# A decoder block on one core: preparation, values and loads of W2 in another order within the turns

## The reference

```python
x = x + attention(layernorm(x))           # 16 heads of 128, softmax over channels
x = x + xattn(layernorm(x), ctx, gamma)   # below
x = x + ffn(layernorm(x))                 # below

# xattn: q is (B, 512, 512), split in 8 heads of 64 rows; k = v = ctx, split the same way
qk = einsum('bhdq,bhdl->bhql', qh, kh) / sqrt(64)
ret = gamma * einsum('bhql,bhdl->bhdq', softmax(qk), vh)

# ffn: w1q, w3q (1365 x 512) and w2q (512 x 1365) are ternary: sign(w) or 0, times mean |w|
out = (silu(x @ w1q.T) * (x @ w3q.T)) @ w2q.T
```

## Time and profile before

| | |
|---|---|
| median of 3 runs | 1131.79 us (1130.19 to 1132.29) |
| the profiled execution | 1132.07 us |
| its span | 1130.2 us |
| mean granted clock of PE | 0.997 |
| busy: PE, PEld | 1111.2 us (98%), 940.3 us (83%) |
| busy: DVE, ACT, POOL | 731.0 us (65%), 542.2 us (48%), 478.3 us (42%) |
| PE's share of the chain that ended last | 89% |

### The profile page before, as it was taken

One profiled execution on the slowest core, in us unless ns is written; L12 is line 12 of the kernel. 1 busy time (PEld: TensorE's weight loads), 2 busy tenths in 40 slices (PEclk: granted clock), 3 DMA queues, 4 the chain that ended last, 5 costly groups with the idle time before them and its releaser, 6 DMA issues.

```text
span 1130.2 us, 15803 instructions
## 1 busy us (share of the span) xinstructions
PE 1111.2 (98%) x5804; PEld 940.3 (83%) x5804; DVE 731.0 (65%) x1357; ACT 542.2 (48%) x1129; POOL 478.3 (42%) x420
## 2 busy tenths in 40 slices
PE   8999999999999999999999999989999999999998
PEld 6888888878888888888888888878787878888886
DVE  7555547777757588866424434679867976787532
ACT  3556673324142376677514323267627753775130
POOL 0222327341332275664434030266627762875131
PEclk9999999999999999999999999999999999999999
DMA  7465553545433634212631022362113211310000
GB/s 242 161 184 188 183 180 122 166 126 172 124 121 126 206 96 141 84 38 94 240 112 45 30 100 61 135 176 65 48 44 114 58 48 57 113 47 2 38 1 37
DMA packets 54663, 122.19 MB, mean 108 GB/s; under 512 B 10057, under 2 KB 10057, under 8 KB 52538
## 3 DMA queue, kind: packets, MB, share of 16 engines
q1 hardware_dynamic: 54586, 121.18, 33.2%
HBM read 103.32 MB, written 17.84 MB: 107 GB/s over the span
## 4 chain that ended last, share of the span: by engine, by line
PE 89%; DVE 4%; POOL 2%; DMA 1%; issue 1%; ACT 1%; SPq 0%; POOLq 0%; DVEq 0%; ACTq 0%
PE bank L161 19%; PE bank L162 19%; PE bank L163 19%; PE bank L562 5%; PE bank L563 5%; PE bank L520 4%; PE bank L577 4%; PE bank L578 4%; PE bank L530 2%; PE bank L544 2%; PE bank L545 2%; PE bank L531 2%; DMA x1d<-x_scratch 1%; POOL kl L909 1%; POOL qst L913 1%
## 5 line engine op out<-in xcount | busy, mean ns | idle before, releaser
L562 PE MATMUL bank<-x3h,w 128*128 128x512 f32 (+2 forms) x368 | 143.0, 392 | 0.4 <-DVE x3l L839 0.3
L563 PE MATMUL bank<-x3l,w 128*128 128x512 f32 (+2 forms) x368 | 140.1, 384 | 0.0
L1419 ACT ACTIVATE yh<-bank 128x512 fp32r<-128x512 f32 x64 | 38.1, 600 | 209.9 <-PE bank L163 209.9
L2025 POOL TENSOR_TENSOR wal<-raw_a,wah 128x512 fp32r<-128x512 f32 x44 | 60.5, 1401 | 137.5 <-ACT wah L1441 137.5
L754 DVE TENSOR_REDUCE xmx<-bank 128x1 f32<-128x512 f32 x128 | 87.6, 686 | 42.7 <-PE bank L531 41.4
L919 POOL TENSOR_SCALAR pe_x<-pe_x,xri,gam 128x512 f32<-128x512 f32 x96 | 75.6, 788 | 88.6 <-DVE xri L758 85.6
L2030 POOL TENSOR_TENSOR wbl<-raw_b,wbh 128x512 fp32r<-128x512 f32 x64 | 87.6, 1393 | 36.1 <-ACT wbh L1462 35.9
L161 PE MATMUL bank<-wah,gh 128*128 128x512 f32 x256 | 102.6, 401 | 0.0
L161 PE MATMUL bank<-yh,rh 128*128 128x512 f32 x256 | 100.2, 391 | 0.8 <-DVE xacc L1887 0.8
L1717 DVE TENSOR_TENSOR yl<-bank,yh 128x512 fp32r<-128x512 f32 x64 | 44.1, 691 | 86.8 <-ACT yh L1419 86.6
L162 PE MATMUL bank<-wal,gh 128*128 128x512 f32 x256 | 100.1, 391 | 0.0
(11 more groups left out here) (168 smaller groups left out, 2990.2 us busy)
## 6 DMA issues: line engine op xcount, KB each, us to landing
raw_a<-in_wk SPq DMA_DIRECT2D x8, 1024.0 KB, 5.6
raw_b<-in_wq SPq DMA_DIRECT2D x8, 1024.0 KB, 6.7
raw_a<-in_wo SPq DMA_DIRECT2D x8, 1024.0 KB, 5.2
raw_b<-in_wvt SPq DMA_DIRECT2D x8, 1024.0 KB, 5.2
ternary_scratch<-wraw SPq DMA_DIRECT2D x24, 341.2 KB, 3.0
x1d<-x_scratch SPq DMA_DIRECT2D x48, 128.0 KB, 2.9
kd<-in_ctx SPq DMA_DIRECT2D x48, 128.0 KB, 2.9
w<-ternary_scratch SPq DMA_DIRECT2D x2, 2730.0 KB, 10.9
```

Source lines behind the costliest of these rows:

```text
L562: pe.matmul(u_bank[w][0:m, cols], lhs, x3h[:, c, cols], start=c == 0, stop=False)
L563: mm = pe.matmul(u_bank[w][0:m, cols], lhs, x3l[:, c, cols], start=False, stop=c == CK - 1)
L2025: pool.tensor_tensor(wal[:, c, :], raw_a[:, c, :], wah[:, c, :].bitcast(F32), ALU.subtract).then_inc(s["wal_pool"], 1)
```

## The change

`prep_step` becomes 4h for all heads: head 3 is prepared at step 8 instead of 9, head 7 at 24 instead of 25, each with its second half (`act_queries`, `pool_prep`) one step later as before. `values_step` becomes 1, 10, 18 and 26 instead of 1, 8, 17 and 24, and POOL's low parts come at 2, 11, 19 and 27. In turn 1, SP issues W2 behind head 2's rows and ahead of the wait for vd. All instructions stay, only their places change.

```diff
         def values_step(h):
-            return 4 * h + (h % 4 == 0)
+            return 4 * h + 2 if h else 1
         def prep_step(h):
-            return 4 * h + (h % 4 == 2) if 0 < h < XH - 1 else None
+            return 4 * h if 0 < h < XH - 1 else None
...
+        def sp_vd(sp, m, b, h):
+            if h or b > 1:
+                sp.wait_ge(s["vtl"], b * V_TILES + h // 2)
+            sp.dma_start(m.vd[:], rows(ctx_cols, b)[h // 2]).then_inc(s["vd_in"], 16)
+
-        def sp_head(sp, m, b, h):
+        def sp_head(sp, m, b, h, values=True):
...
-            if h % 2 == 0 and b > 0:
-                if h or b > 1:
-                    sp.wait_ge(s["vtl"], b * V_TILES + h // 2)
-                sp.dma_start(m.vd[:], rows(ctx_cols, b)[h // 2]).then_inc(s["vd_in"], 16)
+            if h % 2 == 0 and b > 0 and values:
+                sp_vd(sp, m, b, h)
...
-            sp_head(sp, main, 1, 2)
+            sp_head(sp, main, 1, 2, values=False)
             sp_w2(sp)
+            sp_vd(sp, main, 1, 2)
...
-                    if values_step(h // 2 * 2) == n - 1:
-                        pool_vt(pool, main, b, h // 2 * 2)
+                    if n - 1 in map(values_step, range(0, XH, 2)):
+                        pool_vt(pool, main, b, (n - 1) // 8 * 2)
```

## The result

The changed kernel takes 1120.07 us (median of 4 runs, 1119.48 to 1123.63), the kernel before 1131.97 beside it: a ratio of 0.9905, 95% interval 0.9892 to 0.9919, so 11.9 us or 1.1% less. The prediction was 1121.8, with 10.1 us less. The profiled execution has a span of 1118.8 us, 11.4 less than before.

What follows compares the result with a forecast made beforehand. PE, busy 98% of the span, was taken as the bound. Five gaps (5.8 us) plus turn 1 (4.3) made 10.1 us, taking the profiled 1132.07 to 1122.0 and the median to 1121.8; range 1120.0 to 1126.5.

Steps and rivals of the forecast that it cites:

- Part 1: Moving preparation of heads 3 and 7 one step earlier removes five PE gaps before steps 12 and 28: 5.83 us.
- 10.8 us for all that can be removed: Ceiling on the gain: 9.09 us of PE gaps in turns 1 to 3 plus 1.71 us of lower clock.
- What is late next: POOL's second pe_x, moved behind kl, qst and gtl, would be the nearest to delaying PE, with 2.1 us of margin.
- Part 2: Moving the values of heads 4 and 6 to later steps: no PE gap stands there, worth nothing by itself.
- The spare time of head 7's rows: In turn 2, head 7's last load lands at 904.0 and DVE wants it about 906.2: 2.2 us spare.
- slower rival: Head 7's loads land as slowly as head 3's in turn 1 (12.3 us), DVE and PE stand: 1143 us; chance 0.03.
- Part 3: Issuing W2 ahead of the wait in turn 1 shrinks one PE gap, removes another and the clock drop: 4.3 us.
- L: When head 3's rows land in turn 1: 751.4, from 754.26 less 2.9; bounds 750.9 and 753.0.
- standstill rival: W2's landing comes no earlier, DVE and ACT wait longer; turn 1 gives nothing or up to 1.5 us: 1126.0; chance 0.16.
- The sum: Five gaps 5.8 us plus turn 1's 4.3 us give 10.1 us less, a time of 1121.8 us.

## Why the prediction was right, step by step

**Part 1, five gaps, 5.83 us: right in place and cause, too small by 1.4.** All five are gone. The prediction said that a single gap costs nothing more than its idle time, since the product behind it took 0.50 us and not the 0.77 of the lower clock. That was the wrong comparison, and so its 10.8 us for all that can be removed was too low: a gap costs PE more than its idle time. Products overlap: in the profile after the change, one starts at 866.00, lasts 0.40 and the next starts at 866.24, so 0.16 of each is hidden, and a gap's idle time is counted from the end. And the first after a gap is slow. The row behind the gap of turn 2 in the kernel before:

```profile
873.76 0.39 PE L531 MATMUL bank<-kl,qst 128*128 128x512 f32 x1
```

From the L530 at 873.42 to this one it is 0.34 us, where the same pair after the change takes 0.23 (866.24 to 866.47). Together 0.16 + 0.11 = 0.27 per gap, 1.35 for five. The two traces, compared step by step, show it gap by gap: at step 28 of turn 1 the changed kernel gains 1.44 us for 1.28 of idle time, and at step 29 another 0.11. The mis-sized term was thus the gap, taken as its idle time alone.

**What is late next: right in name, wrong in size.** I named the second pe_x as nearest, with 2.1 us. I compared its start with PE's; its end counts. In the trace after it ends at about 866.3 (865.59 and one of two that take 1.53), and PE wants it at about 867.6: 1.3 us. In turn 1, where everything hangs on head 3's late rows, a vts of 1.26 us in front of it doesn't fit, as the two runs with the values' table of before showed. ACT's exchange of copies in step 8 was rightly put at nothing; but those two runs, where the copy of the values stays in step 8 beside that of the keys, show that it would have cost 0.3 to 0.5 us in turn 1.

**Part 2, values, "worth nothing by itself": half right.** With the preparation left where it was, 0.2 us; with it moved, 2.0. My text had costed each part against the kernel before and not against the other part. The spare time of head 7's rows was 5.2 us and not 2.2. I had moved only DVE's request by the 1.26 us won at step 12, though the loads of step 19 move with it; POOL's vts of step 19 comes 1.1 us earlier than I had bounded, as the old vts of step 18 no longer stands before it; and SP issued the loads behind it 0.6 us faster. SP's issues in turn 2 (values of heads 6 and 7, last load of head 7) and DVE's use of it:

```profile
889.75 0.34 SPq L409 DMA_DIRECT2D vd<-in_ctx_cols  x1
...
891.98 0.60 SPq L420 DMA_DIRECT2D kd<-in_ctx  x1
```

```profile
900.15 0.53 DVE L748 TENSOR_SCALAR x1d<-x1d,stx 128x512 f32<-128x512 f32 x1
```

They land near 895.0, about 3.0 us after the last issue, and DVE starts on them at 900.15, without a wait. So the slower rival did not come, with the landing at 3.0 us as in the kernel before.

**Part 3, turn 1, 4.3 us: right in its mechanism, and right to the tenth by some luck.** W2 at 735.71 for 735.6, L = 751.75 for 751.4, the gap 0.75 for 0.64, no drop of the clock. From the start of turn 1 to step 14, PE gains 4.36 us. Three small errors cancel in it: a restart of 0.27 that I had left out, the gap that stayed 0.11 longer, and about 0.1 less for the clock (the run with W2's place alone gains 0.77 + 0.84 = 1.61 us at steps 13 and 14, for the 1.71 that I had counted). The choice between the two bounds of L, 1.28 or about 3 us earlier, fell on the draining of W2: x1d started 2.5 us earlier, though head 3's rows were issued only 1.1 us earlier. The landing at 754.2 that the prediction gave to both heads is that of head 3's second half and head 4's first; the last half of head 4 came at 755.5. The Trainium skill's rule (DMA: Bandwidth & Descriptors, Queues, rings and completion order), that each engine's descriptors are consumed in ring order, agrees with these landings, and with head 3's rows ahead of W2: they took 3.1 us in the kernel before and 3.6 in the changed one, for 12.3 and 10.6 behind it. The standstill rival fell with W2's start. The run with the tables alone is what it describes: turn 1 is 3.1 us longer there than with the W2 edit, but still 1.3 us shorter than before, within the rival's "up to 1.5". Its 1126.0 had counted none of that, nor the restarts, and was too high (1122.45).

**The sum.** 5.83 + 1.35 for the five gaps and 4.36 for turn 1 are 11.54 of the 11.64 us measured in the turns. The kernel's median moved by 11.9 in the first comparison and by 11.1 in the two later ones (1131.87 and 1131.89 to 1120.75). (Its own last subtraction, 1122.0 - 0.28, gives 1121.7 and not 1121.8.) Of the 1.5 us by which the turns beat the 10.1, nearly all is thus the restarts behind the five gaps.

## What to carry to other kernels

Where engines work in a written order, a preparation belongs behind the last thing that it really needs, and not behind a wait for another engine's step: here, with W2 in its new place, the move by one step took 5.9 us off the turns (300.78 to 294.87), clearing POOL of 1.26 us of work in front of it only 0.2 net (to 300.59), and both together 7.9 (to 292.89). When work is put forward on an engine, ask at once what it now stands before, and compare that work's end, not its start, with the moment it is wanted. A large transfer with slack goes behind the small ones that have none, even if its own issue could be earlier: that order took 1.0 us more off the turns (to 291.87). Compare two traces step by step at the busiest engine, and not only the idle time in its waits.

## What the runs showed of the hardware

- A gap in PE's stream cost 0.26 to 0.27 us over its idle time, for the five gaps of about 1.0 to 1.3 us (0.16 of overlap lost, 0.11 in the first product) and for the one of 0.75 (1.02 us in the turns).
- Granted clock, in the two traces that have such a pair: two gaps close together (1.35 and 1.91 us with 3.0 of work between, or 1.17 and 0.93 with 1.2 between) were followed by about 3.3 us at 0.5, the lower level (1.2 GHz), and a loss of about 1.7 us. Single gaps of 0.75 to 1.34 were followed by none, nor were gaps of 0.55 and 1.00 with 4.4 between (granted clock 1.00 throughout, preparation moved and values not).
- Loads of 128 KB issued 1.3 and 7.7 us behind a 2,560 KB one took 12.3 and 7.6 us (medians of two), so that issues 6.4 us apart landed within 3.3 us of each other; ahead of it they took 3.1 and 3.6 us. The large load's own end is not in the traces.
- POOL took up a result of DVE 0.37 us after the start of DVE's reciprocal, which takes 0.15 (866.01 - 865.64).
